# GRU inside a two-layer kernel: the input's product formed for 64 steps at once in float32r, and written by ScalarE into the recurrence's PSUM banks

## What is computed

```python
vz = video @ C_z + b_z        # vr, vh alike
xz = einsum('btd,de->bte', seq, W_z)      # xr, xh alike
def step(h, xs):
    z = sigmoid(xzt + h @ U_z + vz)
    r = sigmoid(xrt + h @ U_r + vr)
    hh = tanh(xht + r * h @ U + vh)
    h_new = (1.0 - z) * h + z * hh
```

## Time and profile before

| | |
|---|---|
| median of three timed runs | 2375.61 us (2373.63 to 2375.72) |
| profiled execution, its own time | 2376.38 us |
| its span, first to last instruction | 2374.5 us |
| mean granted clock | 0.751 |
| TensorE matmuls | 2271.0 us busy (96%), 34421 |
| TensorE weight loads | 2070.6 us (87%), 34421 |
| VectorE | 1536.1 us (65%), 8470 |
| ScalarE | 789.8 us (33%), 3046 |
| GpSimd | 485.3 us (20%), 621 |
| chain that ended last, traced part | matmuls at L1456 17%, L1464 8% (the last stage) |

### The profile page before, as it was taken

The page is one execution under the profiler, slowest core; times in us unless marked ns, Lnnn a source line. Parts: engine busy times, 40 slices in busy tenths (PEclk is TensorE's granted clock), DMA queues, the critical chain, the costliest instruction groups (busy, mean ns, idle before and its releaser), DMA issues. The chain is left out here.

```text
span 2374.5 us, 87150 instructions
## 1 busy us (share of the span) xinstructions
PE 2271.0 (96%) x34421; PEld 2070.6 (87%) x34421; DVE 1536.1 (65%) x8470; ACT 789.8 (33%) x3046; POOL 485.3 (20%) x621
## 2 busy tenths in 40 slices
PE   4999999999999999999899999999999999999997
PEld 3999999999999999998677888866999998899986
DVE  7777777777777777777644455484466665566656
ACT  1222222222222222222555766633222222222221
POOL 4000000000000000000301000144355555455544
PEclk7555555555555555555899999999999999999998
DMA  3000000000000000000102132310787787677772
GB/s 113 4 4 4 4 4 4 4 4 4 4 4 4 4 4 4 4 4 4 37 0 79 36 107 76 126 55 25 274 271 254 259 270 234 226 263 254 265 233 64
DMA packets 55514, 212.99 MB, mean 90 GB/s; under 512 B 11592, under 2 KB 40980, under 8 KB 46996
## 3 DMA queue, kind: packets, MB, share of 16 engines
q1 hardware_dynamic: 35076, 182.64, 20.7%
q0 software_dynamic: 17408, 23.61, 5.4%
q10 hardware_dynamic: 2704, 2.18, 0.3%
HBM read 192.83 MB, written 15.57 MB: 88 GB/s over the span
## 5 line engine op out<-in xcount | busy, mean ns | idle before, releaser
L1456 PE MATMUL bank<-xe,ring 128*128 128x160 f32 x3072 | 452.5, 305 | 0.6 <-ACT xe L1475 0.6
L1456 PEld LDWEIGHTS bank<-xe,ring 128*128 128x128 f32 x3072 | 430.2, 193 | 3.4 <-issue 0.7
L473 PE MATMUL bank<-xs,Ws 128*128 128x64 bf16 x2304 | 403.7, 306 | 9.3 <-DVE vbs L381 9.3
L489 PE MATMUL bank<-keep_part,Us 128*128 128x4 f16 x6132 | 346.5, 173 | 10.3 <-DVE keep_part L417 3.3
L489 PEld LDWEIGHTS bank<-keep_part,Us 128*128 128x128 f16 x6132 | 303.0, 115 | 51.2 <-DVE keep_part L417 3.4
L489 PE MATMUL bank<-h_part,Us 128*128 128x4 f16 x6144 | 329.0, 171 | 0.0
L1501 DVE STREAM_TRANSPOSE turned<-ye 32x64 f32<-32x64 f32 x1280 | 300.4, 235 | 16.7
L489 PEld LDWEIGHTS bank<-h_part,Us 128*128 128x128 f16 x6144 | 290.0, 114 | 8.3
L1516 DVE TENSOR_TENSOR mid<-bank,gate_f 128x160 f32<-128x160 f32 x384 | 117.9, 319 | 227.0 <-ACT gate_f L1484 226.7
L288 ACT ACTIVATE r_h<-bank 128x8 f32<-128x8 f32 x512 | 92.7, 181 | 494.0 <-PE bank L489 494.0
L1419 POOL DMA_INDIRECT out_rows<-res,to_row x128 | 192.0, 1500 | 277.2 <-DVE res L1510 230.7
(11 more groups left out here) (233 smaller groups left out, 3747.3 us busy)
## 6 DMA issues: line engine op xcount, KB each, us to landing
ring<-in_ew SPq DMA_DIRECT2D x64, 2304.0 KB, 8.1
raw<-in_L_cond_ew SPq DMA_DIRECT2D x16, 1024.0 KB, 6.2
ctx_rows<-rows SPq DMA_DIRECT2D x2, 1280.0 KB, 6.7
dense_w<-in_L_ffn_W SPq DMA_DIRECT2D x2, 1024.0 KB, 6.5
raw<-in_L_cond_sw SPq DMA_DIRECT2D x2, 1024.0 KB, 6.2
out_rows<-orow SPq DMA_DIRECT2D x4, 512.0 KB, 3.2
got<-ctx_rows,row POOLq DMA_INDIRECT x128
out_rows<-res,to_row POOLq DMA_INDIRECT x128
```

What stands on the lines that cost most here:

```text
L473: yield lambda o=o_x, g=g, k=k, w=w, x=x, cols=cols, m=m: nc.tensor.matmul(o, Ws[:, g, w, k, cols], xs[:, x, k, :, t0:t0 + SEG], start=(m ...
L489: last = nc.tensor.matmul(pre[g][q][:, jj, m, :], Us[:, g, p, k, m * P:(m + 1) * P], x[part][:, k * B:(k + 1) * B], start=False, stop=Fals ...
L1456: last = nc.tensor.matmul(bank[f % UPS][:, s_ * CAP:(s_ + 1) * CAP], w1[u][:, k, s_ * FFN + f * P:s_ * FFN + (f + 1) * P], xe[u % 2][:, k] ...
```

## The change

The input's product is formed for SPAN = 64 steps at once. W and x are split into two float32r parts each (`W_part`, `x_part`), unscaled; three pairs (`MEET`) and two halves of the contraction make 6 matmuls of 128x128 by 256 columns for each of 6 groups (gate, half of the outputs), 36 for a span in place of 360. They go into two PSUM banks of their own (`xw`, banks 6 and 7), one in each of the steps 0 to 35 of the span before, between the low half of h_part and rh_high. The recurrence's banks now hold 64 steps each (full, 512 words); TensorE sets them up once with a product of zeros (`clear`). ScalarE writes each group into them, scaled and with the bias, one activation for each of the 4 sequences (`seed`, Identity with a per-partition scale and bias, 64 columns, stride of 8 words in PSUM), one behind each of 24 tanh. The first span is written by VectorE instead, before the recurrence. The inputs are split span by span: the high part by ScalarE behind the tanh of step 40, the low part by VectorE at the end of steps 41 and 42; GpSimd no longer splits anything. EARLY is 128 steps. The conditioning term is formed with C as weights, 18 matmuls that include the bias from one partition. W's three loads signal separately; the high part of U and of W is made by ScalarE; the zeroing of VectorE's tiles moves to its front; the `which` tile and its load go. The chain of a step is otherwise as it was. The diff, cut to its core:

```diff
-        EARLY = 4 * SEG
+        SPAN = 64
+        SPANS = S // SPAN
+        EARLY = 2 * SPAN
...
-        rest = t("rest", [P, GATES, KD, D])
         Us = t("Us", [P, GATES, 2, KD, D], F16)
-        Ws = t("Ws", [P, GATES, PARTS, KD, D], BF16)
-        xs = t("xs", [P, PARTS, KD, B, S + SEG], BF16)
-        x_rest = t("x_rest", [P, KD, B, S + SEG])
+        W_part = [t(f"W_part{p}", [P, GATES, KD, D], F32R) for p in range(2)]
+        x_part = [t(f"in_part{p}", [P, KD, B, S], F32R) for p in range(2)]
...
-        which = t("which", [B, SEG * B])
-        which_bf = t("which_bf", [B, SEG * B], BF16)
+        bias = t("bias", [1, GATES, D])
+        vb = t("vb", [P, GATES, KD, B])
+        zeros = t("zeros", [P, 512], BF16)
...
-        FILL = (2, 1, 3)
         PART_OF = ((0, 1), (0,))
-        PAIRS = ((0, 0), (0, 1), (1, 0), (0, 2), (1, 1), (2, 0))
-        pre = [[bank[2 * g + q][:, 0:SEG * C2].rearrange("p (t m b) -> p t m b", t=SEG, m=KD)
-                for q in range(2)] for g in range(GATES)]
+        GROUPS = GATES * KD
+        TERMS = KD * len(MEET)
+        SPLIT_AT = GROUPS * TERMS + B
+        pre = [[bank[2 * g + q][:].rearrange("p (t m b) -> p t m b", t=SPAN, m=KD) for q in range(2)] for g in range(GATES)]
+        xw = [bank[6 + n][:, 0:B * SPAN].rearrange("p (b t) -> p b t", b=B) for n in range(2)]
...
+                def high_inputs(span):
+                    nc.scalar.activation(steps_of(x_part[0], span), steps_of(xT, span), ACT.Copy).then_inc(s_xhi, 1)
...
+                high_inputs(0)
+                for g in range(GATES):
+                    act.wait_ge(s_w[g], 16)
+                    nc.scalar.activation(W_part[0][:, g], W[:, g], ACT.Copy).then_inc(s_whi, 1)
+                high_inputs(1)
                 act.wait_ge(s_scale, 2)
+                for g in range(GATES):
+                    nc.scalar.activation(Us[:, g, 0], U[:, g], ACT.Copy, scale=scale[:, g:g + 1]).then_inc(s_uhi, 1)
...
+                def seed(span, n, b):
+                    g, m = n // KD, n % KD
+                    if b == 0:
+                        act.wait_ge(s_xw, span * GROUPS + n + 1)
+                    nc.scalar.activation(pre[g][span % 2][:, :, m, b], xw[n % 2][:, b], ACT.Identity,
+                                         scale=scale[:, GATES + g:GATES + g + 1], bias=vb[:, g, m, b:b + 1]).then_inc(s_seed, 1)
...
+                    turn = jj - (TERMS - 1)
+                    if span + 1 < SPANS and 0 <= turn < GROUPS * TERMS and turn % TERMS < B:
+                        seed(span + 1, turn // TERMS, turn % TERMS)
+                    if span + 2 < SPANS and jj == SPLIT_AT:
+                        high_inputs(span + 2)
...
-                for first_part, done, steps in ((s_xs, s_xs, slice(0, EARLY)), (s_xl, s_xl, slice(EARLY, S + SEG))):
-                    x, left = xT[:, :, :, steps], x_rest[:, :, :, steps]
-                    part = [xs[:, p, :, :, steps] for p in range(PARTS)]
-                    pool.wait_ge(first_part, 1)
-                    for k in range(KD):
-                        nc.gpsimd.tensor_tensor(left[:, k], x[:, k], part[0][:, k], ALU.subtract).then_inc(done, 1)
-                    for k in range(KD):
-                        nc.gpsimd.tensor_tensor(part[1][:, k], x[:, k], part[0][:, k], ALU.subtract).then_inc(done, 1)
-                    pool.wait_ge(done, 1 + 2 * KD)
-                    for k in range(KD):
-                        nc.gpsimd.tensor_tensor(part[2][:, k], left[:, k], part[1][:, k], ALU.subtract).then_inc(done, 1)
...
+                def low_inputs(span, pieces):
+                    for k in pieces:
+                        nc.vector.tensor_tensor(steps_of(x_part[1], span)[:, k], steps_of(xT, span)[:, k],
+                                                steps_of(x_part[0], span)[:, k].bitcast(F32), ALU.subtract).then_inc(s_xlo, 1)
+
+                def low_weights(g):
+                    dve.wait_ge(s_whi, g + 1)
+                    nc.vector.tensor_tensor(W_part[1][:, g], W[:, g], W_part[0][:, g].bitcast(F32), ALU.subtract).then_inc(s_wlo, 1)
...
+                for n in range(GROUPS):
+                    g, m = n // KD, n % KD
+                    dve.wait_ge(s_xw, n + 1)
+                    nc.vector.scalar_tensor_tensor(out=pre[g][0][:, :, m, :].rearrange("p t b -> p b t"), in0=xw[n % 2],
+                                                   scalar=scale[:, GATES + g:GATES + g + 1],
+                                                   in1=vb[:, g, m].unsqueeze(2).to_broadcast([P, B, SPAN]),
+                                                   op0=ALU.mult, op1=ALU.add).then_inc(s_first, 1)
+                dve.wait_ge(s_xhi, 2)
+                low_inputs(1, range(KD))
...
+                    if span + 2 < SPANS and SPLIT_AT < jj <= SPLIT_AT + KD:
+                        dve.wait_ge(s_xhi, span + 3)
+                        low_inputs(span + 2, (jj - SPLIT_AT - 1,))
...
+                def clear(q):
+                    for g in range(GATES):
+                        last = nc.tensor.matmul(bank[2 * g + q][:], ones_bf[:], zeros[:], start=True, stop=True)
+                    return last
...
+                def input_product(span):
+
+                    for n in range(GROUPS):
+                        g, m = n // KD, n % KD
                         for k in range(KD):
+                            for i, (w, x) in enumerate(MEET):
+                                def one(n=n, g=g, m=m, k=k, i=i, w=w, x=x):
+                                    if k == 0 and i == 0:
+                                        if span == 0:
+                                            if m == 0:
+                                                pe.wait_ge(s_wlo, g + 1)
+                                            if n >= 2:
+                                                pe.wait_ge(s_first, n - 1)
+                                        elif n >= 2:
+                                            pe.wait_ge(s_seed, ((span - 1) * GROUPS + n - 1) * B)
+                                    last = nc.tensor.matmul(xw[n % 2], W_part[w][:, g, k, m * P:(m + 1) * P],
+                                                            x_part[x][:, k, :, span * SPAN:(span + 1) * SPAN],
+                                                            start=(k == 0 and i == 0), stop=(k == KD - 1 and i == len(MEET) - 1))
+                                    if k == KD - 1 and i == len(MEET) - 1:
+                                        last.then_inc(s_xw, 1)
+                                yield one
...
+                for g in range(GATES):
+                    for m in range(KD):
+                        at = (g * KD + m) * B
+                        for k in range(KD):
+                            nc.tensor.matmul(bank[1][:, at:at + B], C[:, g, k, m * P:(m + 1) * P], condT[:, k],
+                                             start=(k == 0), stop=False, skip_group_check=True)
+                        last = nc.tensor.matmul(bank[1][:, at:at + B], bias[:, g, m * P:(m + 1) * P], ones[0:1, 0:B],
+                                                start=False, stop=True, skip_group_check=True)
+                last.then_inc(s_v, 1)
...
+                pe.wait_ge(s_xlo, KD)
+                for f in input_product(0):
                     f()
+                pe.wait_ge(s_vb, 1)
+                pe.wait_ge(s_scale, 1)
+                clear(1)
+                pe.wait_ge(s_ulo, GATES)
+                pe.wait_ge(s_first, GROUPS)
...
-                        fill(jj, 0)
                         pe.wait_ge(s_hlo, m)
                         recur(1, q, jj, state, 1).then_inc(s_zp, 1)
-                        fill(jj, 1)
+                        if jj < len(ahead):
+                            if jj == 0:
+                                pe.wait_ge(s_xlo, (span + 2) * KD)
+                            ahead[jj]()
...
+                            if njj == 0:
+                                pe.wait_ge(s_seed, (span + 1) * GROUPS * B)
                             pe.wait_ge(s_khi, m)
                             recur(0, nq, njj, kept, 0)
-                            fill(jj, 2)
```

More of the change, by code:

```diff
@@ L357, in _ @@
                 nc.vector.tensor_scalar(scale[:, 3 * GATES:], scale[:, 2 * GATES + 1:2 * GATES + 2], -1.0, None, ALU.mult).then_inc(s_scale, 1)
-                dve.wait_ge(s_v, 2)
-                dve.wait_ge(s_vb, 1)
-                nc.vector.tensor_tensor(vb[:, 2], bank[7][0:B, 0:D], bias[:, 2], ALU.add).then_inc(s_wsc, 1)
-                dve.wait_ge(s_wsc, 1)
-                for g in range(GATES):
-                    last = nc.vector.tensor_scalar(vb[:, g], vb[:, g], scale[0:B, GATES + g:GATES + g + 1], None, ALU.mult)
@@ L364, in _ @@
-                last.then_inc(s_vb, 1)
-                dve.wait_ge(s_w, 16 * GATES)
-                for g in range(GATES):
-                    last = nc.vector.tensor_scalar(Ws[:, g, 0], W[:, g], scale[:, GATES + g:GATES + g + 1], None, ALU.mult)
```

(14 more changed lines are left out.)

144 lines of the change are left out of this document (54 added, 90 removed).

## The result

The changed kernel takes 2302.93 us, the median of four runs (2302.56 to 2303.38), where the kernel before takes 2375.3 beside it: a ratio of 0.9697, with a 95% interval of 0.968 to 0.9713. The forecast was 2303 in a range of 2277 to 2332.

A forecast was written before the change was run, and what follows sets the result against it. The prediction took the recurrence's step chain, with product pieces overflowing a gap, as the bound, not TensorE's busy time. Recurrence -52.4, start -20.5, rest 0: -72.9 from the median 2375.6, forecast 2303 us, range 2277 to 2332.

The forecast's parts named there:

- the free steps: Recurrence steps with no piece of the input's product: 1.99 us from gate to gate, expected to stay so.
- the whole overflow: Recurrence: three product pieces between keep_part's halves overflow the second gap, step_high's weights at 1.61 us instead of 1.44.
- Part 1 and 2: Recurrence: small product pieces leave, 77.6 us gained; 252 float32r matmuls ahead of rh_high each delay 0.095 us, +24.0 us.
- Rival B: Gap ahead of rh_high: load takes 0.107 us or is fetched early, all covered, 2279 us; chance 0.12.
- C: Gap ahead of rh_high: nothing of load or stream overlaps, 0.25 us late, 2342 us; chance 0.11.
- D: Gap ahead of rh_high: 256 columns stream in two passes, 0.31 us late, 2357 us; chance 0.03.
- Part 3: ScalarE in the recurrence: 168 seeds and six copies of the inputs' high part fit its idle time, cost 0.
- E: ScalarE: Identity brings two table loads per seed, 2.57 us, 0.4 covered; +364 us, near 2667; chance 0.03.
- Part 4: VectorE, steps 41 and 42: 12 low-input subtractions of about 0.34 us each make r*h 0.1 late, +1.2 us.
- Part 5: Start: GpSimd's splitting leaves, second gate at 29.6 us instead of 50.13, gain 20.5 us, bounds 16 and 24.

The follow-up runs named there:

- bf16_fill: The changed kernel with the input's product held in bfloat16 in place of float32r, less exact: 2282.44 us.
- half_columns: The changed kernel with each product matmul streaming 128 of its 256 columns from span 1 on, float32r load kept: 2280.49 us.
- twice_columns: The changed kernel with each product matmul streaming its 256 columns twice, 512 in all, from span 1 on: 2356.90 us.
- bf16_twice: twice_columns with the product held in bfloat16 in place of float32r: 2301.96 us.
- more_scalar: The changed kernel with two more ScalarE operations of the seed's form behind each of the 168 seeds: 2304.13 us.
- gpsimd_work: The changed kernel with GpSimd making six unused subtractions of 128x1792 elements once the inputs are there: 2317.79 us.
- two_gaps: The changed kernel with each product matmul from span 1 on split into two of 128 columns, one in either gap: 2283.37 us.
- other_gap: The changed kernel with each whole product matmul from span 1 on moved between the two halves of the kept state's product: 2298.75 us.

## Why the prediction was right, and where it was not

**Which bound holds.** Right: the free steps keep the length that they had, 1.986, and the product's pieces gone are worth the whole overflow. Between the second gate and the last, 251 periods have a fill and 259 are free.

**Part 1 and 2, the step.** The chain was right in kind, and confirmed by four runs: bf16_fill, half_columns, twice_columns and bf16_twice. The delay was 0.087 us a fill where I had 0.095: 251 x 0.087 = 21.8 us instead of 24.0. The two numbers inside it were both off. Ahead of rh_high the float32r load costs 0.214 more than a bfloat16 one, hence about 0.24 with the 0.026 that I gave a 16-bit load, not 0.21. With that my own sum would give 0.125; the 0.04 between it and the measurement means that the fill begins to count that much later, or rh_high's matmuls could start that much later without loss, than I read from the rows. One and the same 0.04 fits the float32r fill, the bfloat16 one with 512 columns and the zero delay of the two lighter ones. Which of the two it is was not shown. The rule that I weighed there (the Trainium skill, TensorE: Matmul & The Clock Gate, section LDWEIGHTS) has no type in it, and twice_columns against bf16_twice speaks against it for float32r in this place. Rival B therefore falls, C (nothing overlaps, 2.24) and D (two passes, 2.3) as well.

**Part 3, ScalarE.** Right that the seeds cost nothing: steps 1 to 4, which have none, and 5 to 28, of which four in six have one, have the same 2.073. The cover is larger than the idle time less the record's length, as more_scalar has it. E fell: there is no table load in the recurrence.

**Part 4, VectorE's low inputs.** Wrong, +1.2 us that did not come. The timeline of steps 40 to 41 of span 4:

```profile
639.46 0.17 DVE L446 TENSOR_TENSOR h_part<-ring,h_part 128x8 f16<-128x8 f32 x1
639.54 0.42 DVE L345 TENSOR_TENSOR in_part<-xT,in_part 128x256 fp32r<-128x256 f32 x1
639.88 0.17 DVE L416 TENSOR_TENSOR rh_high<-r_h,ring 128x8 f16<-128x8 f32 x1
```

The gate is at 639.65 and r*h starts 0.23 us later, where it does in every step, although the pass lasts 0.42, longer than my 0.34. It starts 0.09 before the record of the operation ahead of it ends, and the one behind it 0.08 before its own end. I had set a duration against an idle time as if records did not overlap, the same mistake as in my number for more_scalar.

**Part 5, the start.** The cause was right, as gpsimd_work shows, and the size was off: the second gate came at 33.87, not 29.6, 16.3 us gained instead of 20.5, just over the lower bound of 16. The steps that failed, in order: C is used at 12.46 and not at 9.6 (I held that nothing changed in C's landing, while the early load beside it was twice as large); the condition's 36 loads take 21.16 - 12.46 = 8.7 us, 0.24 each and not 0.21, which is again the load term, 1.1 us; from the reading of the scales to the first gate 10.15 us pass and not 9.2. In the product's 24 later matmuls I had allowed for either pace; the executions show both, and the changed kernel has nearly all of them at the slower one (last section).

**Sum.** Start +4.3 (second gate), recurrence 1035.4 against 1038.1, -2.7, the later stages -2.4, of which 1.5 go with the missing fall of the clock: -0.8 together. That 2302.93 lies so near to 2303 is these three cancelling, which is luck. The recurrence's -2.7 is the fill's -2.2, Part 4's -1.2, -0.7 for free steps of 1.983 on average in this execution, and +1.4 for something that I had not foreseen and that is told at the end.

## What to carry to other kernels

Price a filler by the gap it is put in, load and stream together, and fit the size of the piece to the gap: 256 float32r columns cost 22 us, the same columns as two pieces of 128 in two gaps cost nothing, with twice the loads. Float32r weights were dear behind short streams (4 columns, here) and free behind 256 columns; if the precision allows, the 16-bit form gives the same gain. And look into each engine's queue for small products that others wait for (here 6.2 us of VectorE's time behind a long one), but expect a start to pay back only what its longest chain gives up.

## What the runs showed of the hardware that was not expected

- Behind f16 matmuls of 4 columns, a 128x128 float32r weight load cost 0.214 us more than a bfloat16 one at a granted clock of 0.50 (2.287 against 2.073), as much as 256 columns streamed there. Behind matmuls of 256 columns it cost nothing: 0.213 us from one to the next with either type.
- At the start, each VectorE instruction with two SBUF inputs that began well inside one of GpSimd's with two (six in the kernel before, five in gpsimd_work) lasted until that one had ended, however small it was itself: 3.64 us for 128x8. What it costs is the rest of GpSimd's instruction.
- Records of one engine overlap: on ScalarE the next operation starts 0.10 us before the record of a 128x64 one ends, on VectorE 0.08 before that of a 128x256 one. What an operation takes from a gap is the distance to the next start.
- Sixteen steps, every eighth from 240 to 360, are 0.14 us longer than their neighbours (2.127 against 1.987) in the changed kernel and in bf16_fill, two_gaps and others, because step_high starts 0.35 us after the tanh and not 0.21. In fill steps of the changed kernel only 0.05 of it shows, in twice_columns nothing. It costs 1.4 us in the changed kernel and 16 x 0.14 = 2.2 where no fill absorbs it; its cause stays open.
- The same 24 product matmuls of the start took 4.75 us in the changed kernel and 2.96 in bf16_twice, and in bf16_fill and half_columns (timelines):

```profile
25.44 5.25 PE L473 MATMUL bank<-in_part,W_part 128*128 128x256 bf16 x24 [1.55 <-DVE bank L399]
...
25.34 3.29 PE L474 MATMUL bank<-in_part,W_part 128*128 128x256 f32 x24 [1.36 <-DVE bank L399]
```

By single records, the pace changes once in the changed kernel: the starts are 0.213 us apart up to 29.49, the pace of 256 columns at 1.2 GHz, and 0.116 to 0.122 apart from 29.70 on, near that at 2.4 (0.107). The trace's first record of a granted clock is 1.0 from 29.69 on; for the time ahead of it there is none, and the 1.00 that a table of stretches prints there rests on no record. In half_columns that record begins at 24.42, ahead of all 24, in bf16_twice at 23.46, and in bf16_fill at 30.53, behind all but the end of the last. In the other kernels in which the pace changes among the 24, it changes where that record begins too (27.59 in other_gap, 28.31 in more_scalar). So what decides is when the clock rises. Why it rose at these different times stays open. It moved the first gate by up to 2 us.
